# An audio tower on one core: x loaded only in its transposed form, bias by VectorE, more buffers, new instruction orders

## The chip, the cores and the metric

The kernel runs on one core of a Trainium2 chip. The metric is the device time of one execution in microseconds. Three runs of the kernel before gave 224.62, 225.06 and 225.22 us; the median is 225.06 us. The profiled execution took 224.04 us, of which the trace covers a span of 222.3 us.

## What is computed

The input x has 8 sequences of 375 rows of 128 floats. All arithmetic is fp32. Cut to what matters:

```
xt = x^T per sequence
h  = silu(conv1x1(xt, w_compress) + b)             # 128 -> 64 channels
h  = silu(conv3(h, w_main, padding 1) + b)         # 64 -> 64
h  = conv1x1(h, w_expand) + b_expand               # 64 -> 128, the third convolution
y  = layer_norm(h^T + x) * g + b
y  = layer_norm(gelu(y @ w_ff1 + b) @ w_ff2 + b + y) * g + b
h  = max over 3 neighbouring rows                  # 373 rows are left
h  = h + softmax(q k^T) @ n,      n = layernorm(h), q = (n Wq + bq)/sqrt(128), k = n Wk + bk
h  = h + mixture(layernorm(h)):   8 experts 128 -> 256 -> 128 with gelu, the two best of each row,
                                  weighted by a softmax over those two
```

## The kernel before

The work is a set of pieces, each with a name and a number: the number is a sequence (0 to 7), a pair of sequences (0 to 3), or a block. `a1` is the first convolution of a pair, `a2` the second, `a3` the third; `a4` transposes the normalised rows, `a5` and `a6` are the feed-forward part, `a7` transposes back, `mp` is the maximum, `hr` transposes to rows; `b1`, `bq`, `sc0` to `sc2`, `pt0` to `pt2` and `at` are the attention; `h1`, `g1`, `g2`, `g3` the gate of the experts. `l1` to `l4` apply the four layer norms and `p1` to `p4` compute their 1/sqrt on GpSimd.

Three sequences (0, 6, 7) go through all eight experts: `D1` and `D2` are the two products of one expert on TensorE, `dg` the gelu on ScalarE, `da` the weighted sum on VectorE. The five others are sparse. GpSimd scatters their rows (`scat`, 30 indirect DMAs) into a DRAM array by expert, `tab` is the table that tells which 128 rows and which expert each block has, and 37 blocks are computed: SyncE loads the rows (`lx`) and the weights (`lw`, for blocks 8 to 36; `rg` reads one entry of the table into a register first), TensorE transposes (`T`), and multiplies twice (`L1`, `L2`), ScalarE does the gelu (`gl`), VectorE adds the bias (`yv`), and GpSimd scatters the result (`so`). At the end SyncE loads each sparse sequence's results (`yl`), VectorE combines them (`fin`), and SyncE stores (`out`, `od`).

What each engine does next is fixed by five strings, PE_ORDER, DVE_ORDER, ACT_ORDER, POOL_ORDER and SP_ORDER; every engine works through its own string in order and waits on semaphores. In PE_ORDER the figure after the colon is the PSUM bank of the piece. `w.0` to `w.3` are products of the identity with itself whose result nobody reads; WARM says how many (12, 15, 5 and 3). One fp32 matmul shows as two records in the trace (two passes), one transpose as one.

Names that the change touches: x comes in twice, as `xt` (transposed, into `xt_sb`) and as `x` (rows, into `x_sb`, by `load_x` on SyncE's queue). Piece `xb` on GpSimd adds the bias `row_be` of the third convolution to `x_sb` (line 528); piece `a3` on VectorE adds `x_sb` to the convolution's result out of PSUM (line 737). TensorE's `a3` computes a pair of sequences in two banks, 12 matmuls (line 1056). The two lines of SyncE that hold a block's loads back are

```
wait(sp, "T", n - LOADS + 1)            # lx n: ten loads of rows ahead at most
wait(sp, "yv", n + 1 - WSLOTS)          # lw n: seven buffers for weights
```

## Time and profile before

| | before |
|---|---|
| three runs, median (lowest to highest) | 225.06 us (224.62 to 225.22) |
| profiled execution | 224.04 us |
| its span in the trace | 222.3 us |
| TensorE busy | 207.5 us (93%) |
| VectorE busy | 154.3 us (69%) |
| ScalarE busy | 136.8 us (62%) |
| GpSimd busy | 112.7 us (51%) |
| chain that ended last | TensorE 74%, VectorE 8%, ScalarE 5%, DMA 4% |

PE is TensorE's matmuls, PEld its weight loads (which run beside them), DVE VectorE, ACT ScalarE, POOL GpSimd, SPq SyncE's DMA queue. The span falls into a head (0 to about 53 us, the convolutions and the feed-forward part), a middle (53 to 144.75 us, attention and gate), the blocks (144.75 to 199.1 us) and a tail (199.1 us to the end). Idle time of an engine is what stands in brackets in the timeline, with what ended it.

### The profile page before, as it was taken

How to read it: one execution, taken by the hardware profiler on the slowest of the kernel's cores; microseconds unless marked ns; L12 is line 12 of the kernel's file. 1: busy time of each engine (PE TensorE's matmuls, PEld its weight loads, DVE VectorE, ACT ScalarE, POOL GpSimd, SP SyncE). 2: the span in 40 equal slices, each digit the busy share in tenths (PEclk: the TensorE clock that was granted, in tenths of full speed). 3: DMA queues.
4: the chain of work that ended last, by engine and by line, in shares of the span. 5: the costliest groups of instructions: out<-in, count | busy, mean ns of one | idle time of the engine just before them, and what ended most of it. 6: DMA issues, size and time to landing. Idle time of an engine off the chain costs nothing.

```text
span 222.3 us, 5473 instructions
## 1 busy us (share of the span) xinstructions
PE 207.5 (93%) x1575; PEld 170.2 (77%) x1575; DVE 154.3 (69%) x688; ACT 136.8 (62%) x302; POOL 112.7 (51%) x168
## 2 busy tenths in 40 slices
PE   6997897899999999999999999999999799899990
PEld 6875566568956976888779886889998688699780
DVE  6049899999898998988779952486434333234895
ACT  2122988898898588867587446736646366444430
POOL 7608585740541045757774787005777667572000
PEclk9999999999999999999999999999999999999997
DMA  5999999950010002111210121377596889822673
GB/s 152 247 235 288 319 402 406 401 211 3 0 35 0 4 0 69 52 35 58 61 58 25 38 80 48 74 219 251 187 307 225 295 292 322 300 65 76 179 228 105
DMA packets 26000, 35.31 MB, mean 159 GB/s; under 512 B 4083, under 2 KB 18838, under 8 KB 25971
## 3 DMA queue, kind: packets, MB, share of 16 engines
q1 hardware_dynamic: 23137, 30.60, 43.8%
q0 software_dynamic: 2240, 4.00, 5.6%
q10 hardware_dynamic: 594, 0.36, 0.7%
q8 instruction: 13, 0.21, 0.4%
q14 instruction: 16, 0.13, 0.2%
HBM read 10.61 MB, written 14.39 MB: 112 GB/s over the span
## 4 chain that ended last, share of the span: by engine, by line
PE 74%; DVE 8%; ACT 5%; DMA 4%; issue 3%; SPq 3%; POOL 1%; DVEq 0%; ACTq 0%
PE PS L1189 11%; PE PS L1182 10%; PE PS L1124 7%; PE PS L1106 7%; PE PS L1214 5%; PE PS L1001 5%; PE PS L1205 5%; DMA blk_x<-xs 4%; PE PS L989 4%; PE PS L1113 4%; PE PS L1101 3%; PE PS L1018 2%; DVE acc L965 2%; DVE x_sb L930 2%; PE PS L1198 2%
## 5 line engine op out<-in xcount | busy, mean ns | idle before, releaser
L517 POOL TENSOR_TENSOR rstd<-mv,mhalf 125x3 f32<-125x3 f32 x32 | 27.6, 865 | 43.9 <-DVE mv L698 43.7
L547 POOL DMA_INDIRECT ys<-yblk,blk_x x37 | 35.9, 971 | 27.2 <-DVE yblk L956 19.2
L661 ACT ACTIVATE gd<-PS,bias 128x373 f32<-128x373 f32 x48 | 27.0, 573 | 15.4 <-PE PS L1182 10.8
L541 POOL DMA_INDIRECT xs<-rows_x,pos_x x30 | 29.9, 995 | 13.0 <-issue 8.4
L1182 PE MATMUL PS<-xt_sb,w_all 128*128 128x373 f32 x96 | 35.7, 482 | 0.0
L1189 PEld LDWEIGHTS PS<-w_all,gd 128*125 128x125 f32 x288 | 33.6, 187 | 2.1
L1189 PE MATMUL PS<-w_all,gd 128*125 128x128 f32 x288 | 34.6, 273 | 0.0
L672 ACT ACTIVATE gb_t<-PS,blk_w 128x128 f32<-128x128 f32 x58 | 18.0, 364 | 13.3 <-issue 6.9
L930 DVE SCALAR_TENSOR_TENSOR x_sb<-PS,comb,x_sb 125x128 f32<-125x128 f32 x72 | 20.7, 343 | 5.8 <-PE PS L1189 4.9
L1182 PEld LDWEIGHTS PS<-xt_sb,w_all 128*128 128x128 f32 x96 | 15.7, 190 | 5.0 <-issue 0.9
L956 DVE TENSOR_TENSOR yblk<-PS,blk_w 128x128 f32<-128x128 f32 x29 | 8.4, 290 | 15.0 <-PE PS L1214 13.4
L1106 PE MATMUL PS<-xn_t,q_t 128*125 128x373 f32 x48 | 17.7, 486 | 0.0
L1124 PE MATMUL PS<-xn,prob_t 125*125 125x129 f32 (+1 forms) x144 | 17.6, 275 | 0.0
L1214 PE MATMUL PS<-blk_w,gb_t 128*128 128x128 f32 x116 | 17.4, 277 | 0.0
L1205 PE MATMUL PS<-xb_t,blk_w 128*128 128x128 f32 x116 | 17.3, 276 | 0.0
L1124 PEld LDWEIGHTS PS<-xn,prob_t 125*125 125x125 f32 (+1 forms) x144 | 16.7, 187 | 0.8 <-issue 0.4
L1205 PEld LDWEIGHTS PS<-xb_t,blk_w 128*128 128x128 f32 x116 | 15.6, 191 | 1.8 <-issue 0.3
L817 DVE COPY xb_t<-PS 128x128 f32<-128x128 f32 x27 | 7.8, 289 | 13.0 <-PE PS L1198 10.7
L1214 PEld LDWEIGHTS PS<-blk_w,gb_t 128*128 128x128 f32 x116 | 15.0, 191 | 0.7 <-issue 0.3
L831 DVE TENSOR_REDUCE nmax<-PS 125x1 f32<-125x373 f32 x24 | 12.8, 544 | 2.6 <-PE PS L1106 1.8
L637 ACT ACTIVATE prob_t<-PS 124x373 f32<-124x373 f32 (+1 forms) x23 | 9.9, 482 | 6.0 <-PE PS L1113 5.8
L631 ACT ACTIVATE prob<-PS,nmax 125x373 f32<-125x373 f32 x24 | 12.5, 572 | 1.5 <-DVE nmax L831 1.2
(201 smaller groups left out, 416.2 us busy)
## 6 DMA issues: line engine op xcount, KB each, us to landing
blk_w<-w_all SPq DMA_DIRECT2D x29, 321.0 KB, 3.2
xs<-blank SPq DMA_DIRECT2D x1, 8256.0 KB, 25.9
blk_x<-xs SPq DMA_DIRECT2D x37, 64.5 KB
yg<-ys SPq DMA_DIRECT2D x5, 336.0 KB
x_sb<-in_x SPq DMA_DIRECT2D x4, 336.0 KB
out<-x_sb SPq DMA_DIRECT2D x8, 168.0 KB
xt_sb<-in_xt SPq DMA_DIRECT2D x3, 375.0 KB, 6.2
w_all<-in_we SPq DMA_DIRECT2D x1, 1024.0 KB
```

The lines of the kernel that those rows point to most:

```text
L517: pool.tensor_tensor(rstd[i][:, n % 2, :], mv[i][:, n % 2, :, 1], mhalf[:], ALU.pow)\
L541: pool.indirect_dma_start(xs, bass.IndirectOffsetOnAxis(ap=pos_x[:, b // 2, s, i:i + 1], axis=0), rows_x[:, k, s, j, :], None, bounds_chec ...
L547: pool.indirect_dma_start(ys, bass.IndirectOffsetOnAxis(ap=blk_x[n % SLOTS][:, t, D:XW].bitcast(u32), axis=0), yblk[n % YBUF][:, t, :], No ...
L661: act.activation(gd[:, k % GD, c, 0:TP], of("D1", n)[:, 0:TP], ACT.Gelu, bias=bias128[:, 2 + k % E * HC + c:3 + k % E * HC + c]).then_inc( ...
L672: last = act.activation(gb_t[n % 2][:, c, :], of("L1", n)[:, c * BLK:(c + 1) * BLK], ACT.Gelu, bias=w[:, 2 * H + c:2 * H + c + 1])
L930: last = dve.scalar_tensor_tensor(flat(h2[:, b, :])[j], flat(of("D2", n)[0:P, :])[j], w[:, j, b % 2, e:e + 1], flat(h2[:, b, :])[j], ALU.m ...
L1106: pe.matmul(f[0:P, 0:TP], q_t[:, s, OFF[j]:OFF[j] + P], xn_t[:, s, :], start=True, stop=True)\
L1124: last = pe.matmul(f[0:P, j * (D + 1):(j + 1) * (D + 1)], prob_t[0:ROWS[c], s, c, OFF[j]:OFF[j] + P], xn3[0:ROWS[c], s, c, :], start=(c == ...
L1182: pe.matmul(f[:, 0:TP], w_all[:, k % E, c * 128:(c + 1) * 128], x32[:, DENSE[k // E], 0:TP], start=True, stop=True).then_inc(S["D1"], 1)
L1189: last = pe.matmul(f[0:P, j * D:(j + 1) * D], gd[:, n % GD, c, OFF[j]:OFF[j] + P], w_all[:, n % E, H + c * D:H + (c + 1) * D], start=(c == ...
L1205: last = pe.matmul(f[:, c * BLK:(c + 1) * BLK], w[:, c * 128:(c + 1) * 128], xb_t[n % 2][:], start=True, stop=True)
L1214: last = pe.matmul(f[:, t * D:(t + 1) * D], gb_t[n % 2][:, c, t * 128:(t + 1) * 128], w[:, H + c * D:H + (c + 1) * D], start=(c == 0), sto ...
```

## The change

x is no longer loaded as rows. `load_x`, `x_sb` and the GpSimd piece `xb` are gone. TensorE's `a3` now begins with six transposes (three for each sequence of the pair) that put x as rows into the two banks, and the 12 matmuls of the convolution accumulate onto them. VectorE adds the bias `row_be` instead of `x_sb`. The attention's result goes into a tile `h2` of its own.

The room is used for more buffers: 14 for the blocks' weights instead of 7 (seven of them lie in a tile `late` that also holds the attention's `prob` and `prob_t`, so the first load into it waits for the last attention product), 12 for the blocks' results instead of 6, and five for the final loads instead of three, so that `yl` no longer waits for `fin`. WARM goes from (12, 15, 5, 3) to (5, 12, 2, 2). All five orders are new. The code also gets pieces by which ScalarE and GpSimd could take over a `fin`, but no order contains them.

```diff
-WSLOTS = 7
-YBUF = 6
+WSLOTS = 14
+OWN = 7
+YBUF = 12
...
 PE_ORDER = """
-w.0:0 a1.0:5 w.1:0 ft.0:7 a2.0:6 a2.1:3 w.2:0 a3.0:1 a3.1:4 a1.1:3 cb.0:2 w.3:0 a2.2:7 a2.3:6 fn.0:0 a1.2:1 bf.0:4
...
+w.0:0 a1.0:4 w.1:2 a2.0:0 a2.1:1 cb.0:6 ft.0:3 w.2:4 a3.0:2 a3.1:5 a1.1:3 a1.2:6 bf.0:1 a2.2:7 a2.3:4 fn.0:0 w.3:2
...
 POOL_ORDER = """
-xb.0 xb.1 p1.0 p1.1 xb.2 xb.3 xb.4 p1.2 xb.5 p1.3 p1.4 p2.0 p2.1 xb.6 xb.7 p1.5 p1.6 p2.2 p2.3 p3.0 p3.1 p1.7 p2.4
...
+p1.0 p1.1 p1.2 p1.3 p2.0 p2.1 p1.4 p1.5 p1.6 p2.2 p2.3 p3.0 p3.1 p1.7 p2.4 p2.5 p4.0 p2.6 p3.2 p4.1 p3.3 p2.7 p3.4
...
 SP_ORDER = """
-rg.22 rg.23 rg.24 rg.25 rg.26 lx.0 lx.1 lx.2 lx.3 lx.4 lx.5 lx.6 lx.7 lx.8 lw.8 lx.9 lw.9 lx.10 lw.10 lx.11 lw.11
...
+c4.1 c4.2 c4.3 c4.4 rg.8 rg.9 rg.10 lw.8 lw.9 rg.11 rg.12 rg.13 rg.14 rg.15 c4.5 rg.16 lw.10 lw.11 lw.12 rg.17 rg.18
+rg.19 lx.0 lx.1 lx.2 rg.20 rg.21 lx.3 lx.4 lx.5 lx.6 rg.22 lw.13 lx.7 lx.8 lw.14 lx.9 lx.10 rg.23 lx.11 lw.15 lw.16
...
-WARM = (12, 15, 5, 3)
+WARM = (5, 12, 2, 2)
...
-        x_sb = sb("x_sb", [P, B, NJ * D])
...
-        prob = sb("prob", [P, 2, NJ, TP])
+        late = sb("late", [128, (WSLOTS - OWN) * WROW])
+        prob = late[0:P, 0:2 * NJ * TP].rearrange("p (s j t) -> p s j t", s=2, j=NJ)
...
-        prob_t = sb("prob_t", [P, 2, NJ, TE])
-        h2 = x_sb
+        prob_t = late[0:P, 2 * NJ * TP:2 * NJ * (TP + TE)].rearrange("p (s j t) -> p s j t", s=2, j=NJ)
+        h2 = sb("h2", [P, B, NJ * D])
...
             sp.dma_start(xt_sb[:, 0, :], xt[:, 0, :]).then_inc(s_xt[0], 16)
             sp.dma_start(wc_p[:], wc).then_inc(S["wc"], 16)
+            load_xt(1)
             for s in range(2):
                 sp.dma_start(we_d[HALF[s], :], we).then_inc(S["we"], 16)
-            load_x(sp, 0)
-            load_xt(1)
...
-            load_x(sp, 1)
             for q in range(2, Q):
                 load_xt(q)
-                load_x(sp, q)
...
                 if name == "lw":
                     k = n - E
                     if k == 0:
                         sp.wait_ge(S["be1"], 1)
+                    if k == OWN:
+                        wait(sp, "at", B)
...
                 if name == "yl":
-                    if n >= YG:
-                        wait(sp, "ob", n - YG + 1)
...
-                if name == "xb":
-                    pool.wait_ge(s_x[n // 2], 32)
-                    v = x_sb[:, n, :].rearrange("p (j d) -> p j d", j=NJ)
-                    pool.tensor_tensor(v, v, row_be[:].unsqueeze(1).broadcast_to([P, NJ, D]), ALU.add)\
-                        .then_inc(S["xb"], 1)
...
                 if name == "a3":
                     wait(dve, "a3", n + 1)
-                    wait(dve, "xb", n + 1)
+                    if n == 0:
+                        dve.wait_ge(S["rows"], 16)
                     wait_nth(dve, "n1", n - 2)
-                    dve.tensor_tensor(r1[:, n % 2, :], of("a3", n)[0:P, 0:NJ * D], x_sb[:, n, :], ALU.add)\
+                    dve.tensor_tensor(r1[:, n % 2, :].rearrange("p (j d) -> p j d", j=NJ),
+                                      of("a3", n)[0:P, 0:NJ * D].rearrange("p (j d) -> p j d", j=NJ),
+                                      row_be[:].unsqueeze(1).broadcast_to([P, NJ, D]), ALU.add)\
                         .then_inc(S["r1"], 1)
...
                     fs = [claim(name, n - 1, ("r1", n)), claim(name, n, ("r1", n + 1))]
+                    for i in range(2):
+                        for j in range(NJ):
+                            pe.matmul(fs[i][0:P, j * D:(j + 1) * D],
+                                      xt_sb[:, n - 1 + i, :].rearrange("d (p j) -> d j p", j=NJ)[:, j, :], ident[:],
+                                      start=(j == 0), stop=False, is_transpose=True)
                     for j in range(NJ):
                         for i in range(2):
                             for half in range(2):
                                 m = HROWS[half]
                                 last = pe.matmul(fs[i][half * HP:half * HP + m, j * D:(j + 1) * D],
                                                  hc2[HALF[half ^ i], n - 1 + i, j, 0:m], we_d[HALF[half ^ i], :],
-                                                 start=True, stop=True)
+                                                 start=False, stop=(j == NJ - 1))
```

The start of TensorE's order before: the idle products (`PS0<-ident`) stand ahead of the first convolution, ahead of the second, and ahead of the third.

```order
L1001 MATMUL PS0<-ident 128x128 x12
L1007 MATMUL PS5<-xt_sb,wc_p 64x375 x2
L1001 MATMUL PS0<-ident 128x128 x15
L1039 MATMUL PS7<-ident,wk_sb 128x128
L1040 MATMUL PS7<-ident,wq_sb 128x128
L1018 MATMUL PS6<-hc1,wm_d 64x192 x2
...
L1001 MATMUL PS0<-ident 128x128 x5
L1056 MATMUL PS1<-we_d,hc2 64x128
```

The same place now, as far as the first product of the third convolution.

```order
L1026 MATMUL PS0<-ident 128x128 x5
L1032 MATMUL PS4<-xt_sb,wc_p 64x375 x2
L1026 MATMUL PS2<-ident 128x128 x12
L1043 MATMUL PS0<-hc1,wm_d 64x192 x2
...
L1051 MATMUL PS6<-ident,rows6 128x6
L1064 MATMUL PS3<-ident,wk_sb 128x128
L1065 MATMUL PS3<-ident,wq_sb 128x128
L1026 MATMUL PS4<-ident 128x128 x2
L1079 MATMUL PS2<-ident,xt_sb 125x128 x3
L1079 MATMUL PS5<-ident,xt_sb 125x128 x3
L1086 MATMUL PS2<-we_d,hc2 64x128
```

Five, twelve and two idle products are left of twelve, fifteen and five; the transposes of the two weight matrices moved behind the second convolution, and six transposes of `xt_sb` stand ahead of the third.

GpSimd's order at its start before: the bias additions (`x_sb<-x_sb,row_be`) among the 1/sqrt of the first layer norm (`rstd`).

```order
L528 TENSOR_TENSOR x_sb<-x_sb,row_be 125x384 x2
L517 TENSOR_TENSOR rstd<-mv,mhalf 125x3 x2
L528 TENSOR_TENSOR x_sb<-x_sb,row_be 125x384 x3
L517 TENSOR_TENSOR rstd<-mv,mhalf 125x3
L528 TENSOR_TENSOR x_sb<-x_sb,row_be 125x384
L517 TENSOR_TENSOR rstd<-mv,mhalf 125x3
```

The same place now.

```order
L530 TENSOR_TENSOR rstd<-mv,mhalf 125x3 x4
L534 TENSOR_TENSOR nrs<-rstd,minus 125x3
L536 TENSOR_TENSOR nmr<-mv,nrs 125x3
L530 TENSOR_TENSOR rstd<-mv,mhalf 125x3
L534 TENSOR_TENSOR nrs<-rstd,minus 125x3
```

Nothing but the layer norms' small operations is left there.

SyncE's order before, at the first loads of the blocks (`blk_x<-xs` are rows, `blk_w<-w_all` weights, `tab_x` an entry of the table).

```order
L436 DMA blk_x7<-xs 128x129
L436 ISA
L436 DMA blk_x8<-xs 128x129
L444 ISA
L444 DMA blk_w0<-w_all 128x642
L436 ISA
L436 DMA blk_x9<-xs 128x129
L444 ISA
L444 DMA blk_w1<-w_all 128x642
```

SyncE's order now, a little ahead of the first load of rows.

```order
L460 DMA blk_w2<-w_all 128x642
L460 ISA
L460 DMA blk_w3<-w_all 128x642
L460 ISA
L460 DMA blk_w4<-w_all 128x642
L436 TENSOR_LOAD tab_x
...
L450 DMA blk_x0<-xs 128x129
L450 DMA blk_x1<-xs 128x129
L450 DMA blk_x2<-xs 128x129
```

Five loads of weights now stand ahead of the first load of rows, where all of them stood behind the ninth.

## Rows read from the trace of the kernel before

**Rows 1.** Windows: us, then PE, PEld, DVE, ACT, POOL busy, clock, DMA share, GB/s
```profile
15.30:53.17 37.87, 33.53 (x320) 23.18 (x320) 36.12 (x154) 30.07 (x58) 21.81 (x34) 1.00 0.91 306
53.17:144.75 91.58, 91.34 (x614) 73.17 (x612) 73.09 (x371) 67.14 (x134) 46.55 (x60) 1.00 0.14 39
144.75:199.10 54.35, 51.76 (x403) 46.95 (x403) 23.87 (x86) 29.84 (x94) 33.88 (x35) 1.00 0.76 251
```

**Rows 2.** Timeline of the start: start, us, engine, line, operation, idle before
```profile
1.28 0.42 SPq L390 DMA_DIRECT2D wc_p<-in_wc  x1
2.04 5.45 PE L1001 MATMUL PS<-ident 128*128 128x128 f32 x24 [2.04 <-DVE comb_t L712]
2.47 1.41 ACTq L557 DMA_DIRECT2D wm_d<-in_wm  x2
7.43 0.85 PE L1007 MATMUL PS<-xt_sb,wc_p 128*64 128x375 f32 x4
8.21 3.62 PE L1001 MATMUL PS<-ident 128*128 128x128 f32 x30
11.97 1.21 PE L1018 MATMUL PS<-hc,wm_d 64*64 64x192 f32 x24
13.24 0.96 ACT L581 ACTIVATE hc<-PS,bias 128x192 f32<-128x192 f32 x2 [4.28 <-PE PS L1018]
14.42 0.89 PE L1056 MATMUL PS<-we_d,hc 64*64 64x128 f32 x24
```

**Rows 3.** DMA issues: KB each, median us from issue to landing
```profile
wc_p<-in_wc SPq DMA_DIRECT2D x1, 32.0 KB, 3.0
wm_d<-in_wm ACTq DMA_DIRECT2D x2, 48.0 KB, 4.8
```

**Rows 4.** Timeline at 18 to 23 us, VectorE and GpSimd
```profile
18.18 0.82 DVE L704 TENSOR_SCALAR n<-r,mv,rstd 125x128 f32<-125x128 f32 x3
19.17 2.90 POOL L528 TENSOR_TENSOR x_sb<-x_sb,row_be 125x384 f32<-125x384 f32 x3
19.24 2.92 DVE L704 TENSOR_SCALAR n<-r,mv,rstd 125x128 f32<-125x128 f32 x3
```

**Rows 5.** Chain that ended last, pieces: start, us, what
```profile
20.18 1.99 DVE n L704 x2
44.72 0.11 PE PS L1076
170.59 5.03 DMA blk_x<-xs
```

**Rows 6.** Timeline, TensorE where it waits for a block's rows
```profile
175.67 0.33 PE L1198 MATMUL PS<-ident,blk_x 128*128 128x128 f32 x1 [1.40 <-DMA blk_x<-xs]
```

**Rows 7.** Timeline, SyncE's queue among the blocks
```profile
160.01 0.43 SPq L436 DMA_DIRECT2D blk_x<-xs  x1
161.33 0.45 SPq L436 DMA_DIRECT2D blk_x<-xs  x1
166.62 0.51 SPq L444 DMA_DIRECT2D blk_w<-w_all  x1
168.93 0.35 SPq L436 DMA_DIRECT2D blk_x<-xs  x1
192.57 0.58 SPq L444 DMA_DIRECT2D blk_w<-w_all  x1
```

**Rows 8.** Timeline, GpSimd: first and two neighbouring scatters of results
```profile
150.56 0.97 POOL L547 DMA_INDIRECT ys<-yblk,blk_x  x1 [11.91 <-DVE yblk L956]
167.25 0.97 POOL L547 DMA_INDIRECT ys<-yblk,blk_x  x1 [0.30 <-issue]
168.53 0.97 POOL L547 DMA_INDIRECT ys<-yblk,blk_x  x1 [0.30 <-issue]
```

**Rows 9.** Timeline of the tail, VectorE
```profile
207.06 0.87 DVE L930 SCALAR_TENSOR_TENSOR x_sb<-PS,comb,x_sb 125x128 f32<-125x128 f32 x3 [0.45 <-PE PS L1189]
218.87 0.87 DVE L971 SCALAR_TENSOR_TENSOR x_sb<-yg,w_top,acc 125x128 f32<-125x128 f32 x3
```

More of the change, by code:

```diff
@@ L89 @@
+D1.45:1 D2.21:6 D1.46:7 D1.47:4 D2.22:5 D2.23:7
 """
 DVE_ORDER = """
[L91 to L94 removed]
@@ L345, in wait_nth, with summed, gathered, shares @@
                 wait(eng, *nth(name, n))
+        def summed(n):
+            return ("obp", 2 * RANK_POOL["fin", n]) if ("fin", n) in RANK_POOL else ("ob", RANK_DVE["fin", n])
+        def gathered(eng, n):
+            s, loads = s_yl[n]
+            eng.wait_ge(s, loads + 32)
+        def shares(n):
+            return w_top[:, SPARSE[n] // 2, :, :].rearrange("p s (j b) -> p s j b", b=2)[:, :, :, SPARSE[n] % 2:SPARSE[n] % 2 + 1]
         def normed_by(i, n):
@@ L376, in audio_tower @@
         block = ctx.enter_context(nc.Block())
-        def load_x(eng, q):
-            for lo, hi in SPLIT:
-                eng.dma_start(x_sb[lo:hi, 2 * q:2 * q + 2, :],
-                              x[2 * q:2 * q + 2].rearrange("b (p j) d -> p b (j d)", j=NJ)[lo:hi]).then_inc(s_x[q], 16)
         @block.sync
@@ L612, in _ @@
                                    scale=cols[:, 4:5]).then_inc(S[nth("y2", n)[0]], 1)
+                if name == "fm":
+                    gathered(act, n)
+                    w = shares(n)
+                    for s in range(2):
+                        for j in range(NJ):
+                            last = act.activation(flat(yg[n][:, s, :])[j], flat(yg[n][:, s, :])[j], ACT.Copy,
+                                                  scale=w[:, s, j, :])
+                    last.then_inc(S["fm"], 1)
                 if name == "hv":
```

172 lines of the change are left out of this document (90 added, 82 removed).

## Prediction

> **What bounds the kernel now.** I read the busy shares first, then the busy time in stretches, then the chain that ended last, then the timelines at the places where TensorE is idle. TensorE is busy 91.34 of the 91.58 us from 53 us to the blocks. It idles in four places: 2.04 us at the very start [rows 2], 37.87 - 33.53 = 4.34 us in the rest of the head, 54.35 - 51.76 = 2.59 us among the blocks [rows 1], and in the tail, which VectorE ends. Not all of what it does is work. The idle products stand on the chain: 24 records take 5.45 us and 30 take 3.62 us before the second convolution can begin [rows 2]. So an edit counts if it takes something off TensorE, removes one of those waits, or shortens the tail.
>
> **The start.** The first 24 records are spaced 5.45 / 24 = 0.227 us, the next 30 are spaced 3.62 / 30 = 0.121 us. The clock column of the windows says 1.00 for both, but the spacing halves: the engine ran at its lower level of 1.2 GHz from its first instruction until the first convolution began at 7.43, and at 2.4 GHz after it [rows 2]. Now the steps.
> - w.0 has 5 products, 10 records: 10 x 0.227 = 2.3 us, over at 4.3. The weights of the first convolution are issued at 1.28 and land 3.0 us later, at 4.3 [rows 2, 3], and xt at about 4.1. So a1.0 starts near 4.4 instead of 7.4. At the lower clock its 0.78 us (8.21 - 7.43) double to 1.6: over at 6.0.
> - w.1 has 24 records. I take the clock to rise at the same time as before, about 7.5: 7 records at 0.227 (1.6 us) and 17 at 0.121 (2.1 us), over at 9.6. The weights of a2 (issued 2.47 to 3.9, the second about 3.2, landing 4.8 later [rows 2, 3]) are there at 8.0. So a2 starts at 9.6, not 11.97: 2.4 us earlier.
> - After a2 (1.21 us, to 10.8) come three transposes and w.2 with 4 records, about 0.8 us together, beside ScalarE's 0.96 us [rows 2]; the third convolution starts at 11.8. Its six transposes cost 6 x 0.11 [rows 5] = 0.7 us, the products 0.89: it ends at 13.4. Before, it ended at 14.42 + 0.89 = 15.3. Gain so far 1.9 us.
>
> **The lock at 19 us.** VectorE's l1.1 takes 2.92 us, where the same three operations took 0.82 just before; the stretch is exactly that of three bias additions on GpSimd, 19.17 to 22.07 [rows 4]. It is on the chain with 1.99 us [rows 5], and a transpose, the second pair's convolution and ScalarE's work are queued behind it. With xb gone, 2.92 - 0.82 = 2.1 us go. VectorE's new operand, row_be, replaces x_sb in an operation of the same shape that reads PSUM; I cost it at nothing. Bounds: it could lose or gain as much as those operations themselves, 8 x 0.1 us, on an engine that is busy 36.12 of the head's 37.87 us [rows 1].
>
> **What the head pays.** 18 more transposes, 18 x 0.11 = 2.0 us of TensorE in the other three pairs; l2.0 moves from VectorE to ScalarE, which stands on the chain there; w.3 gives 2 records back. There are 4.3 us of waits to hide this in, of which some 1.5 us go with the lock, an estimate from the chain's 1.99 [rows 5]. I take half as exposed: 1.0 us lost, bounds 0 and 2.5. What is late next there is ScalarE, with the gelus and their table loads. The trace has no transposing product whose stationary operand is read with a step of three floats, as x now is. The nearest row is the transpose of contiguous columns at 0.11 us; with a load that takes twice as long it would be 0.22 us, so the 24 cost between 2.6 us and 5.3 us, and less than nothing is excluded since they are added work. I take 0.11, the only row there is.
>
> The Trainium skill speaks against that value: by "SBUF — State Buffer", section "Door 1: The DMA port swizzle", SBUF is read in lines of 16 bytes, full bandwidth wants two hits in a line, and every crossing costs; a step of 12 bytes crosses at almost every element. If it holds for weight loads, the doubled price is nearer. No row of the trace decides it.
>
> **The middle (53 to 144.75 us).** TensorE has 0.24 us of idle time there [rows 1] and the same instructions after the change, only in another order. Nothing is taken off, so a gain carried in stays. I cost the new order at 0, bounds -1 and +1 (VectorE is busy 73.09 of the 91.58 us, so a bad order can open a gap).
>
> **The blocks.** TensorE's gaps come from loads of rows that were issued late: 5.03 us from issue to TensorE [rows 5], with 1.40 us of idle in the largest case [rows 6]. They are issued late because SyncE's queue is nearly full: a pair of loads, rows and weights, takes 161.33 - 160.01 = 1.32 us, and two reads of the table between 166.62 and 168.93 take some 1.6 [rows 7], 0.6 to 0.8 each. Its waits on yv for a weight buffer come on top. With 14 buffers these waits fall away, and five weight loads and twelve table reads stand ahead of lx.0, in a time in which SyncE waited for the last scatter anyway. But the work of that queue from lx.0 on stays: 37 + 24 loads at 0.66 = 40.3 us, 17 table reads at 0.65 = 11.1, od.0 with three stores 1.1, together 52.5. Before, its last load of weights was issued at 193.15 [rows 7], 48.4 us after the blocks began. It starts some 5 us ahead of them, so it is at once the next limit: TensorE's own work is 51.8 us [rows 1], GpSimd's 37 scatters at 168.53 - 167.25 = 1.28 are 47.1 us plus the first 6 us [rows 8]. All three lie within 2 us of each other. Of 2.59 us I take 2.0 as gained, bounds 0 and 2.6. The wait for the last attention product ahead of the first load into `late` queues nothing: that product is over before the blocks begin.
>
> **The tail.** After the last L2, TensorE has 9 D2 and 9 D1 before, and 8 and 11 now; da.19 comes at the same distance. From there VectorE works without a gap, 207.06 to 219.7 [rows 9], and has the same da and fin in the new order. yl no longer waits for fin, but no fin waited for yl. I cost it at 0, bounds -0.5 and +0.5.
>
> **The sum.** 1.9 + 2.1 - 1.0 + 0 + 2.0 + 0 = 5.0 us. Against the profiled execution: 224.0 - 5.0 = 219.0. The median of the runs is 1.0 above that execution, so I forecast a median of 220.0 us. With the bounds: the least gain is 1.9 + 2.1 - 2.5 - 1 + 0 - 0.5 = 0, the most 1.9 + 2.1 + 1 + 2.6 + 0.5 = 8.1.
>
> **Rivals.**
> - *The clock rises late.* With 14 fewer records ahead of a1 the engine has done less when the clock used to rise. If all of w.1 runs at 0.227, it ends at 6.0 + 24 x 0.227 = 11.4, the third convolution at 15.2: the start gives 0.1 instead of 1.9, and the time is 221.8. For it: 24 records and no fewer preceded the rise in the one trace there is [rows 2]. Against: the engine is just as continuously busy now, and time passes equally. By the Trainium skill, "TensorE: Matmul & The Clock Gate", section "What's actually happening", the default is the lower clock and continued activity releases it, whatever the number of matmuls; that is for the forecast. The same page ("Part 4: PE-mode transpose") says that transposes do not count as activity.
> - *SyncE's queue is the bound of the blocks.* Then the 2.0 us don't come, since 52.5 us of issue remain behind lx.0 and a new wait for DMA takes the place of the old one: 222.0. For it, the sum above; against it, that the queue starts earlier relative to TensorE and waits nowhere.
> - *More hides.* The transposes fall into waits and all of the 2.59 us go, and the head's gain is the sum of 1.9 and 2.1, perhaps with a shorter path through ScalarE: 225.1 - 6.6 - 1 = 217.5.
> - *Slower: the strided transposes.* One mechanism: each of the 24 stands on TensorE ahead of a convolution that VectorE waits for. It decides from a price at which they eat the 5.0 us: 0.11 + 5.0 / 24 = 0.32 us each. At 0.4 us, the time is 220.0 + 24 x 0.29 = 227. Against it: the visible weight loads of any kind are under 0.2 us.
> - *The change doesn't do what it says*: the lock stays because GpSimd's small 1/sqrt operations take it too. Against it, l1.0 took 0.82 us [rows 4] although GpSimd computes such a 1/sqrt after every norm; it would cost the 2.1: 222.1.
>
> **Chances.** Forecast (about 219 to 221) 0.40; more hides 0.22; SyncE's queue 0.15; late clock 0.11; lock stays 0.03; strided transposes or a bad gap in the middle, slower than before 0.06; the rest, several small losses, near 224, 0.03. The range from 216.8 to 223.0 leaves out the slower cases and the end of the better ones. A measurement of this kernel can tell about 0.3%, 0.7 us, from no change. Faster by more than that (below 224.4) 0.91, within it 0.03, slower 0.06.
>
> **What would show it.** In the trace after: a1's records at 4.4 us and a2's below 10; the spacing of w.1's records falling from 0.23 to 0.12 inside the piece; three operations of l1.1 at about 0.8 us; the first third convolution ending near 13.4, with its transposes at 0.11 us each; TensorE at the first attention product (53.17 before) about 3.0 us earlier; the first block's transpose about 3 us earlier; no idle over 0.5 us before a block's transpose. Wrong would be: gaps of TensorE on VectorE between 60 and 140 us, SyncE's last weight load less than 4 us earlier, or transposes spaced over 0.2 us.

## The result, and the profile after

The changed kernel takes 223.39 us (median of 13 runs, 222.28 to 224.02), the kernel before beside it 224.62 (13 runs, 223.84 to 227.36): ratio 0.9927, 95% interval [0.9902, 0.9953]. It is faster by 0.7%: 1.2 us in the median and 0.8 in the profiled executions (223.23 against 224.04), where 5.0 were forecast; the time lies outside the forecast range. Medians here and below are over all executions, ratios over those within 1.5% of the fastest of their kernel, so the two can differ.

The start came as forecast. The timeline of TensorE after, which answers to [rows 2] (start, us, engine, line, operation, count, idle before):

```profile
4.45 1.52 PE L1032 MATMUL PS<-xt_sb,wc_p 128*64 128x375 f32 x4
5.90 3.69 PE L1026 MATMUL PS<-ident 128*128 128x128 f32 x24
9.52 1.21 PE L1043 MATMUL PS<-hc,wm_d 64*64 64x192 f32 x24
...
11.79 1.30 PE L1079 MATMUL PS<-ident,xt_sb 128*125 128x128 f32 x6
13.02 0.88 PE L1086 MATMUL PS<-we_d,hc 64*64 64x128 f32 x24
```

The second convolution (a2) starts at 9.52 instead of 11.97. The six new transposes ahead of the third one take 1.30 us; 0.7 were costed. They are spaced (13.02 - 11.79) / 6 = 0.205 us. Their line in the trace after, and the line of the other transposes, which read neighbouring columns, in the trace before (duration in ns as min/median/max, first and last start):

```profile
L1079 PEld LDWEIGHTS PS<-ident,xt_sb x24: 246/258/261, 11.8 to 31.9; 128*125 128x125 f32 x24
```

```profile
L1076 PEld LDWEIGHTS PS<-ident,xt_sb x24: 183/187/188, 26.9 to 59.9; 128*125 128x125 f32 x24
```

Both load 125 columns of 128 partitions in fp32. The one with a step of three floats takes 258 ns, the other 187. The long addition of [rows 4] is gone: VectorE's two groups of three now take 0.82 and 0.86 us (timeline after).

```profile
17.83 0.86 DVE L728 TENSOR_SCALAR n<-r,mv,rstd 125x128 f32<-125x128 f32 x3
```

The blocks after, beside the third of [rows 1] (windows: us, then PE, PEld, DVE, ACT, POOL busy, clock, DMA share, GB/s):

```profile
142.80:196.30 53.50, 50.69 (x401) 46.18 (x400) 23.12 (x80) 30.73 (x100) 33.10 (x34) 1.00 0.71 228
```

TensorE is idle there for 53.50 - 50.69 = 2.81 us, against 2.59 before: that wait didn't go. The two ends of the stretch don't stand at the same work as in [rows 1], since TensorE's order has changed around them (the first block's transpose now stands ahead of the piece `bd.1`, and `D2.15` ahead of the last `L2`). So the whole is compared between two points that have the same work behind them in both, but for one piece of three transposes in another's place: the first attention product and VectorE's addition for da.19. The first of them (timelines of TensorE, before and after):

```profile
53.01 2.16 PE L1124 MATMUL PS<-xn,prob_t 125*125 125x129 f32 x18
```

```profile
52.09 2.16 PE L1154 MATMUL PS<-xn,late 125*125 125x129 f32 x18
```

The head gives 0.92 us, although 2.45 had come in. From there to da.19 (207.06 before in [rows 9], 205.83 after) TensorE has 1081 records in both (windows, before and after):

```profile
53.01:207.06 154.05, 151.22 (x1081) 127.73 (x1080) 100.79 (x471) 99.86 (x234) 82.50 (x97) 1.00 0.37 117
```

```profile
52.09:205.83 153.74, 150.85 (x1081) 127.79 (x1080) 100.62 (x474) 98.82 (x236) 83.40 (x96) 1.00 0.37 117
```

That is 0.31 us less, and the idle time in it is the same: 2.83 us before, 2.89 after. Where it sits among the blocks (timeline of TensorE after, blocks' transposes), and pieces of SyncE's queue, its first load of a block's rows, two later ones and its last load of weights, which answer to [rows 7]:

```profile
186.81 0.33 PE L1228 MATMUL PS<-ident,blank 128*128 128x128 f32 x1 [1.65 <-DMA blank<-xs]
189.02 0.33 PE L1228 MATMUL PS<-ident,blank 128*128 128x128 f32 x1
189.85 0.33 PE L1228 MATMUL PS<-ident,blank 128*128 128x128 f32 x1 [0.50 <-DMA blank<-xs]
```

```profile
138.75 4.50 SPq L450 DMA_DIRECT2D blk_x<-xs  x7
...
186.32 1.95 SPq L450 DMA_DIRECT2D blank<-xs  x2
...
192.25 0.50 SPq L460 DMA_DIRECT2D blk_w<-w_all  x1
```

SyncE issues one thing after the other from its first load of a block's rows at 138.75 us to the last load of weights at 192.25: 53.5 us, in which its waits show none. The queue was nearly as full before: from 140.03 to 192.57 us, 52.5 us, with one wait for a weight buffer (SyncE's waits: us in total, times, longest):

```profile
SPq L444 <- DVE yblk L956: 1.5, 1, 1.5
```

So more buffers had 1.5 us of this queue to save, and the new order put more into the same stretch than it took out: 17 reads of the table instead of 10 and three stores (`od`), for five loads of weights fewer. The chain that ended last runs through SyncE's queue from 178.23 to 187.94 us after.

The tail is as before, 1.2 us earlier: the product for da.19 is added at 205.83 (207.06 in [rows 9]), the last row of the output sums starts at 217.65 (218.87). The end of the span moved by 0.8 only, from 222.3 to 221.5; the last stores took 0.4 us longer in this execution.

### The profile page after: what moved, and what is told of

Its sections match the earlier page's. It is cut to its first block, busy times and chain, and to the rows that moved or that the text cites. A ratio compares the mean times of both kernels' runs of the same rounds, so it can differ in the third digit from the quotient of the medians.

```text
span 221.5 us, 5446 instructions
## 1 busy us (share of the span) xinstructions
PE 208.4 (94%) x1571; PEld 170.8 (77%) x1571; DVE 151.5 (68%) x688; ACT 135.8 (61%) x302; POOL 104.6 (47%) x156
## 4 chain that ended last, share of the span: by engine, by line
PE 79%; DVE 10%; SPq 4%; issue 2%; ACT 1%; DMA 1%; POOL 1%; DVEq 0%
PE PS L1219 12%; PE PS L1212 11%; PE PS L1154 7%; PE PS L1136 7%; PE PS L1235 6%; PE PS L1244 6%; PE PS L1014 4%; PE PS L1143 4%; PE PS L1026 3%; PE PS L1131 3%; PE PS L1079 2%; DVE acc L991 2%; DVE h L957 2%; DVE stat L717 2%; SPq L436 2%
## 5 line engine op out<-in xcount | busy, mean ns | idle before, releaser
L562 POOL DMA_INDIRECT ys<-yblk,blk_x x21 | 20.4, 974 | 19.7 <-DVE yblk L983 15.7
L957 DVE SCALAR_TENSOR_TENSOR h<-PS,comb,h 125x128 f32<-125x128 f32 x72 | 20.8, 344 | 6.8 <-PE PS L1219 5.8
L562 POOL DMA_INDIRECT ys<-yblk,blank x16 | 15.6, 974 | 7.0 <-issue 4.0
L1154 PEld LDWEIGHTS PS<-xn,late 125*125 125x125 f32 (+1 forms) x144 | 16.8, 187 | 1.2 <-issue 0.5
L1154 PE MATMUL PS<-xn,late 125*125 125x129 f32 (+1 forms) x144 | 17.4, 274 | 0.0
L661 ACT ACTIVATE late<-PS 124x373 f32<-124x373 f32 (+1 forms) x22 | 9.6, 481 | 7.6 <-PE PS L1143 7.5
L655 ACT ACTIVATE late<-PS,nmax 125x373 f32<-125x373 f32 x24 | 12.5, 571 | 1.9 <-DVE nmax L858 1.8
L696 ACT ACTIVATE gb_t<-PS,late 128x128 f32<-128x128 f32 x28 | 8.6, 365 | 6.5 <-issue 2.8
L696 ACT ACTIVATE gb_t<-PS,blk_w 128x128 f32<-128x128 f32 x30 | 9.4, 365 | 4.9 <-PE PS L1244 2.5
L717 DVE BATCH_NORM_STATS2 stat<-h 125x6 f32<-125x128 f32 x48 | 10.7, 279 | 0.1
```

Source lines behind the costliest of these rows:

```text
L562: pool.indirect_dma_start(ys, bass.IndirectOffsetOnAxis(ap=blk_x[n % SLOTS][:, t, D:XW].bitcast(u32), axis=0), yblk[n % YBUF][:, t, :], No ...
L696: last = act.activation(gb_t[n % 2][:, c, :], of("L1", n)[:, c * BLK:(c + 1) * BLK], ACT.Gelu, bias=w[:, 2 * H + c:2 * H + c + 1])
L717: dve.bn_stats(stat[i][:, j, 0:6], src[j]).then_inc(s_st[i], 1)
L957: last = dve.scalar_tensor_tensor(flat(h2[:, b, :])[j], flat(of("D2", n)[0:P, :])[j], w[:, j, b % 2, e:e + 1], flat(h2[:, b, :])[j], ALU.m ...
L1154: last = pe.matmul(f[0:P, j * (D + 1):(j + 1) * (D + 1)], prob_t[0:ROWS[c], s, c, OFF[j]:OFF[j] + P], xn3[0:ROWS[c], s, c, :], start=(c == ...
```

## The experiments

Runs of one group share a chip and the runs of the kernel before beside them. The first group (four kernels) fell on a chip where the kernel before takes 225.25 us (223.78 to 228.75, 16 runs), like the chip of the result. The other four groups fell on chips where the same kernel before takes 250.16, 249.63, 250.94 and 250.70 us; what the engines do there from 93 us on is told at the end. Up to that point the traces of all chips agree to 0.1 us once the clock's rise is taken out, so the head is read in all of them and whole times only against the kernel before of the same group.

### The price of the step, and of the transposes

The first edit lets the 24 transposes read neighbouring columns.

```diff
-  xt_sb[:, n - 1 + i, :].rearrange("d (p j) -> d j p", j=NJ)[:, j, :], ident[:],
+  xt_sb[:, n - 1 + i, j * P:(j + 1) * P], ident[:],
```

> The changed kernel, but the 24 transposes of x read 125 neighbouring columns instead of every third one, so the third convolution gets the rows of x in a wrong order; same instructions, same sizes. Theory (the step of three floats makes the weight load slow: 24 transposes at 0.21 us instead of 0.11, and most of the 2.3 us is exposed in the head): spacing 0.11 us, the first attention product 1.5 to 2.3 us earlier than at 52.25, and 1 to 2 us off the total of 223.4, since SyncE's queue then starts earlier too. Rival (what the head loses is the new order of ScalarE and VectorE, and the transposes stand beside it): spacing 0.11 us but the attention product within 0.5 us of 52.25 and the total within 0.5 us.

Measured: 221.47 us (6 runs, 220.97 to 223.31), ratio to before 0.9871 [0.9821, 0.9922]. The weight loads take 187 ns, and six transposes 0.92 us instead of 1.30 (timeline of TensorE):

```profile
8.63 1.21 PE L1043 MATMUL PS<-hc,wm_d 64*64 64x192 f32 x24
10.90 0.92 PE L1079 MATMUL PS<-ident,xt_sb 128*125 128x128 f32 x6
...
49.70 2.16 PE L1154 MATMUL PS<-xn,late 125*125 125x129 f32 x18
```

The first attention product stands at 49.70 where the same view of the changed kernel has 52.09 (the chain dates it 0.16 later). Not all of these 2.4 us belong to the edit: a2 starts 0.9 us earlier here, with the same instructions ahead of it, because the 24 idle products took 2.94 us and not 3.69. The clock rose earlier. So from here on the head is measured from the start of a2 to the first attention product: 52.09 - 9.52 = 42.57 us in the changed kernel, 49.70 - 8.63 = 41.07 in this one. The step costs 1.50 us, 24 x 0.063; all of it is exposed.

What this kernel gains in the head also comes out at the end: da.19 is added at 203.56, 2.27 us earlier than in the changed kernel. SyncE's queue starts and ends earlier by as much (136.32 for 138.75, 189.92 for 192.25):

```profile
136.32 4.67 SPq L450 DMA_DIRECT2D blk_x<-xs  x7
...
189.92 0.50 SPq L460 DMA_DIRECT2D blk_w<-w_all  x1
```

The second edit drops the transposes; the third convolution opens the bank itself, and x is left out of the sum.

```diff
-  for i in range(2):
-      for j in range(NJ):
-          pe.matmul(fs[i][0:P, j * D:(j + 1) * D], xt_sb[...], ident[:],
-                    start=(j == 0), stop=False, is_transpose=True)
...
-                     start=False, stop=(j == NJ - 1))
+                     start=True, stop=True)
```

> The changed kernel without the 24 transposes of x; the third convolution's result goes on without x. Theory: all 24 x 0.21 = 5 us of TensorE go, of which the head shows 3 to 4 us at the first attention product (VectorE and ScalarE are next), and the total falls 2 to 3.5 us, no more since SyncE's queue binds the blocks. Rival (the transposes are hidden): total within 0.7 us.

Measured: 222.74 us (11 runs, 220.56 to 224.93), ratio 0.9882 [0.9842, 0.9923]. In the head it is the shortest: 48.17 - 9.00 = 39.17 us. So 24 transposes with the step cost 3.40 us, 24 without it 1.90; the forecast had 1.7 in its two places. On TensorE itself they take 24 x 0.205 = 4.9 and 24 x 0.142 = 3.4 us, so in both cases 1.5 us of them fell into waits. And yet this kernel is only 0.5 us shorter in span than the changed one (221.0 against 221.5), though its first attention product came 3.9 us earlier. Most of what it gave back stands among the blocks (timeline of TensorE, then of SyncE's queue):

```profile
183.72 0.61 PE L1239 MATMUL PS<-late,gb_t 128*128 128x128 f32 x4
186.96 0.85 PE L1223 MATMUL PS<-ident,blank 128*128 128x128 f32 x2 [2.63 <-DMA blank<-xs]
187.61 1.06 PE L1230 MATMUL PS<-xb_t,late 128*128 128x128 f32 x4
```

```profile
134.88 4.22 SPq L450 DMA_DIRECT2D blk_x<-xs  x7
...
182.52 2.13 SPq L450 DMA_DIRECT2D blank<-xs  x2
...
189.03 0.50 SPq L460 DMA_DIRECT2D blk_w<-w_all  x1
```

SyncE again needs 189.03 - 134.88 = 54.2 us from its first load to its last. Its first load came 3.9 us earlier than in the changed kernel, its last 3.2, and the two loads of rows at 182.52 are 3.8 us ahead of the same ones there (186.32). So the queue kept nearly all of the gain; what came late was the data. TensorE could use the first of the two 4.4 us after its issue (186.96 - 182.52), in the changed kernel 2.7 us after it (189.02 - 186.32). Why it landed late isn't shown. TensorE waited 2.63 us, and then ran four products in 1.06 us that had taken 0.61: the granted clock was 0.50 from 188 to 190 us. From the first attention product to da.19 this kernel takes 155.95 us, 2.2 more than the changed one (windows):

```profile
48.17:204.12 155.95, 152.50 (x1081) 129.44 (x1080) 100.65 (x475) 98.83 (x236) 83.29 (x96) 0.99 0.36 113
```

Of these 2.2 us, 0.56 are idle time (3.45 against 2.89) and 1.65 are the same products taking longer. In the tail VectorE then waited 0.8 us for its final loads. This is one execution; the kernel's eleven lie between 220.56 and 224.93 us.

### SyncE's queue

The 29 reads of the table of rows are replaced by the numbers that they give for these inputs. It is no kernel to use, since the numbers hold for these inputs alone, but every transfer stays as it is.

```diff
+FIXED = [CAP * e + BLK * (k + 1) for e, m in enumerate((1, 0, 8, 9, 0, 6, 3, 0)) for k in range(m)] + 2 * [ROWS_X - BLK]
...
-  row_of_block[n] = sp.value_load(tab_x[0:1, n - E:n - E + 1], min_val=0, max_val=ROWS_X - BLK)
+  row_of_block[n] = FIXED[n - E]
```

> The changed kernel, with the 29 reads of the block table on SyncE replaced by the numbers that stand in the table for these inputs. All DMAs stay the same. Theory (the blocks are bound by the number of things SyncE issues one after another): SyncE's last weight load is issued 5 us or more earlier than 192.3, TensorE's 2.8 us of idle among the blocks go, total 2 to 2.8 us lower. Rival (the blocks are bound by what the DMA engines move, 0.71 to 0.8 of them being busy): idle before the blocks' transposes stays over 2 us, total within 0.7 us.

Measured: 219.33 us (6 runs, 218.74 to 219.77), ratio 0.9752 [0.9711, 0.9792], so 4.0 us less than the changed kernel by the two ratios. The head is the changed one (51.84 - 9.27 = 42.57 us). Among the blocks the idle time is gone (windows; the second line is from the first attention product to da.19), and SyncE has time (its queue, and its waits up to 181.7 us as us in total, times, longest):

```profile
142.80:196.30 53.50, 53.45 (x428) 49.53 (x429) 23.95 (x84) 32.27 (x103) 34.90 (x36) 1.00 0.70 227
51.84:202.22 150.38, 150.19 (x1081) 127.79 (x1080) 100.66 (x475) 98.76 (x236) 83.31 (x96) 1.00 0.37 119
```

```profile
138.45 3.61 SPq L451 DMA_DIRECT2D blk_x<-xs  x7
...
181.71 0.47 SPq L461 DMA_DIRECT2D blk_w<-w_all  x1
```

```profile
SPq L451 <- DMA xs<-rows_x,pos_x: 11.8, 1, 11.8
SPq L461 <- DVE yblk L984: 3.0, 5, 1.7
SPq L451 <- PE PS L1229: 3.0, 6, 0.9
SPq L376 <- DMA ys<-yblk,blk_x: 2.0, 2, 1.6
```

From the first attention product to da.19 it is 150.38 us instead of 153.74, 3.36 less, of which 2.70 are idle time (0.19 for 2.89). The rest of the 4.0 is the clock's earlier rise (0.25) and 0.4 us of stores at the very end. First load to last load is 43.3 us instead of 53.5, although SyncE now waits 8.0 us in it, for VectorE, TensorE and GpSimd's scatters: its own work fell from 53.5 to 35.3 us. The edit removes more than the 17 reads behind the first load: with constants, the register operations that work out each load's address go as well, so the 18.2 us are the price of both. Ahead of the first load SyncE waits 11.8 us for the last scatter, where the changed kernel's waited 1.8. So the reads filled the time before the blocks as well.

Both edits together:

> Both edits: transposes of neighbouring columns, and no table reads on SyncE. Theory: the two gains add, 3.5 to 4.8 us below the changed kernel, which would be what the forecast missed. Rival (either bound hides behind a third, GpSimd's scatters at 1.28 us a block): less than 2.5 us together.

Measured: 217.69 us (6 runs, 217.42 to 217.97), ratio 0.9678 [0.9639, 0.9716]: 0.0074 under the constants alone, 1.7 us, which agrees with the 1.50 of the step. With the table reads in place the step had been worth 0.0056, 1.3 us; the intervals don't tell these two apart. TensorE has no idle time in 142.80 to 196.30 (53.50 busy). The two losses add up. At 0.9678 this kernel is some 7 us faster than the kernel before, more than the 5.0 that the forecast expected of the change itself.

### The parts of the head, on the kernel before

Only the shorter idle products:

```diff
-WARM = (12, 15, 5, 3)
+WARM = (5, 12, 2, 2)
```

> The kernel before with the changed kernel's idle products alone (5, 12, 2 and 2 instead of 12, 15, 5 and 3). If the earlier start is worth what the changed trace shows there, the first convolution begins near 4.5 us, the second near 9.5, the first third convolution ends near 13.0 instead of 15.3, and the first attention product stands near 51 instead of 53.2: median near 223. If the later waits of the head (the 2.9 us addition beside GpSimd, ScalarE's gelus) are set by something other than TensorE's start, the first attention product stays within 0.7 us of 53.2 and the median near 224.8.

Only the additions on GpSimd taken away, x left out:

```diff
-  pool.wait_ge(s_x[n // 2], 32)
-  v = x_sb[:, n, :].rearrange("p (j d) -> p j d", j=NJ)
-  pool.tensor_tensor(v, v, row_be[:].unsqueeze(1).broadcast_to([P, NJ, D]), ALU.add).then_inc(S["xb"], 1)
+  continue
...
-  dve.tensor_tensor(r1[:, n % 2, :], of("a3", n)[0:P, 0:NJ * D], x_sb[:, n, :], ALU.add)
+  dve.tensor_tensor(r1[...], of("a3", n)[...], row_be[:].unsqueeze(1).broadcast_to([P, NJ, D]), ALU.add)
```

> The kernel before without GpSimd's eight additions of the bias to x; VectorE adds the bias row to the product instead, and x itself is left out of the sum. If the 2.9 us operation at 19 us is a collision with those additions, it falls to 0.8 us and the first attention product comes 1.5 to 2 us earlier: median near 223. If the chain through ScalarE takes over there, the operation is short but the first attention product moves less than 0.7 us: median near 224.7.

Both:

> Both of the edits above: fewer idle products, and no additions on GpSimd (x left out of the sum). It is the changed head without its transposes. If the two gains add up, the first attention product stands near 49.5 us and the median near 221. If they cover the same time, it stands near 51 and the median near 223. The difference to the changed kernel's 52.25 us is what 24 strided transposes cost in the head: 2.7 us or more by the theory that they are exposed at 0.20 us each, 1.3 or less by the forecast's 0.11 us half hidden.

Whole times, on a chip with the kernel before at 250.16 us: 246.89 (12 runs), ratio 0.9979 [0.9927, 1.003]; 247.32 (12), 0.9986 [0.9937, 1.0036]; 243.29 (8), 0.9845 [0.9783, 0.9907]. The intervals are too wide for the totals to decide; the heads are exact. The starts of a2 and of the first attention product, in the timelines of these three in turn:

```profile
9.85 1.21 PE L1018 MATMUL PS<-hc,wm_d 64*64 64x192 f32 x24
...
50.72 2.16 PE L1124 MATMUL PS<-xn,prob_t 125*125 125x129 f32 x18
```

```profile
11.51 1.21 PE L1019 MATMUL PS<-hc,wm_d 64*64 64x192 f32 x24
...
51.20 2.16 PE L1125 MATMUL PS<-xn,prob_t 125*125 125x129 f32 x18
```

```profile
9.01 1.21 PE L1019 MATMUL PS<-hc,wm_d 64*64 64x192 f32 x24
...
48.53 2.16 PE L1125 MATMUL PS<-xn,prob_t 125*125 125x129 f32 x18
```

| kernel | a2 starts | first attention product | between |
|---|---|---|---|
| before | 11.97 | 53.01 | 41.04 |
| before, idle products as changed | 9.85 | 50.72 | 40.87 |
| before, no additions on GpSimd | 11.51 | 51.20 | 39.69 |
| before, both | 9.01 | 48.53 | 39.52 |
| changed | 9.52 | 52.09 | 42.57 |
| changed, neighbouring columns | 8.63 | 49.70 | 41.07 |
| changed, no transposes | 9.00 | 48.17 | 39.17 |

The additions cost 41.04 - 39.69 = 1.35 us, and 40.87 - 39.52 = 1.35 again beside the other edit. VectorE's operation itself fell from 2.92 to 0.86 us in both (timeline of the second of these kernels):

```profile
18.77 0.86 DVE L701 TENSOR_SCALAR n<-r,mv,rstd 125x128 f32<-125x128 f32 x3
```

Only 1.35 of these 2.06 us reached the path because TensorE had the second pair's convolution to do in the meantime. Before, it then waited 1.28 us for this operation; without the additions it doesn't wait (timelines of TensorE, before and this kernel):

```profile
20.05 0.88 PE L1056 MATMUL PS<-we_d,hc 64*64 64x128 f32 x24
22.21 0.54 PE L989 MATMUL PS<-ident,n 125*128 125x125 f32 x3 [1.28 <-DVE n L704]
```

```profile
20.40 0.54 PE L990 MATMUL PS<-ident,n 125*128 125x125 f32 x3
```

The column adds up: 41.04 - 0.17 (shorter w.2 and w.3) - 1.35 (additions gone) - 0.35 (the rest, the new orders and l2.0 on ScalarE, from 39.52 to 39.17) + 1.90 (24 transposes) + 1.50 (their step) = 42.57.

### The kernel before without its table reads

This is the constants' edit on the kernel before.

> The kernel before with its 29 reads of the table of rows replaced by the same numbers as constants. If SyncE's queue was already the bound of the blocks before, most of TensorE's 2.6 us of idle time there goes and the median is near 222.5. If the waits for a weight buffer set it (9 buffers), the reads fall into those waits and the median stays within 0.7 us of the kernel before.

> Again the kernel before with its 29 reads of the table replaced by constants, beside the others on one chip. If SyncE's queue bounded the blocks before too, TensorE's 2.6 us of idle time there falls under 1 us and the median is near 222.5 (ratio 0.988). If the waits for a weight buffer, with 9 of them, set it, the ratio is over 0.997.

> The kernel before with its 29 reads of the table replaced by constants, once more. If SyncE's queue bounded the blocks before too, TensorE's 2.6 us of idle time there falls under 1 us and the ratio is near 0.988. If the waits for a weight buffer, with 9 of them, set it, the ratio is over 0.997.

> The kernel before with its 29 reads of the table replaced by constants. If SyncE's queue bounded its blocks, its idle time of 2.6 us there falls under 1 us and the ratio is 0.985 to 0.99. If the waits for one of its 9 weight buffers do, over 0.997. On a chip that takes 250 us for the kernel before, the ratio is 0.98 to 0.99 as in the last groups.

Measured on four chips: 0.9829 [0.9734, 0.9923], 0.9888 [0.9821, 0.9956], 0.9801 [0.9715, 0.9886] and 0.9772 [0.9693, 0.9851] (246.14, 245.55, 249.66 and 245.92 us, 6, 12, 6 and 7 runs). All four intervals lie below 1, so the reads and addresses cost the kernel before 1 to 2% as well. But all four chips are of the kind that takes 250 us, and how the gain comes about there isn't shown: in the profiles taken on them, with the reads or without, TensorE waits for no block's rows at all, and SyncE waits for one of its seven weight buffers (the expectations say nine) for 8.9 us in the kernel with the shorter idle products and for 16.9 in the first one with constants. On a chip that takes 225 us this edit wasn't seen, and what it does to the 2.6 us of idle time stays open.

### A version without both losses and without constants

The step can be had for nothing. The host lays xt out with the time steps of one residue side by side; the transposes then read neighbouring columns, and ScalarE puts the order back when it evicts the first convolution.

```diff
-  "xt": a(x, 2, 0, 1),
+  "xt": a(np.asarray(x).reshape(B, P, NJ, D), 3, 0, 2, 1).reshape(D, B, T),
...
-  act.activation(hc1[:, n % 2, 1:T + 1], of("a1", n)[:, 0:T], ACT.Silu, bias=bias64[:, 0:1])
+  act.activation(hc1[:, n % 2, 1:T + 1].rearrange("c (p j) -> c p j", j=NJ),
+                 of("a1", n)[:, 0:T].rearrange("c (j p) -> c p j", j=NJ), ACT.Silu, bias=bias64[:, 0:1])
```

> The changed kernel with xt laid out so that the time steps of one residue (mod 3) are neighbours: the 24 transposes read contiguous columns, and ScalarE's first activation of each pair reads its input with a step of 125 floats instead, to put the order back. Output as the reference's. If the step of 12 bytes in the stationary load is what the transposes paid for, they are spaced 0.11 us, the first attention product comes about 2 us earlier than in the changed kernel (near 50.2), and the median is 1.5 to 2 us under the changed kernel's (near 221.5, ratio to before near 0.985), as with the run on neighbouring columns. If the strided read only moves its price to ScalarE's first activation (0.96 us before), that operation grows and the gain is under 0.7 us.

> The changed kernel with xt laid out by residue, once more. In the head it was 1.5 us shorter than the changed kernel, at the same instruction order. If that reaches the end, the median is 1.5 us under the changed kernel's and the ratio near 0.986. If SyncE's queue, which starts its block loads only 2 us after the last scatter allows, holds the blocks, part of it goes: ratio near 0.991.

The queue can be relieved by issuing the rows of the first eight blocks, whose addresses are fixed, in two transfers.

```diff
+  if n < E:
+      if n in GROUP:                      # {0: (0, 2), 2: (2, 8)}
+          lo, hi = GROUP[n]
+          sp.dma_start(first8[:, lo:hi, :], xs.rearrange("(n r) d -> r n d", n=E)[0:BLK, lo:hi, :])\
+              .then_inc(s_bx[lo], 16)
+      continue
```

> The changed kernel with the loads of rows of the first eight blocks, whose addresses are fixed, issued as two DMAs (blocks 0 and 1, blocks 2 to 7) instead of eight. If what SyncE issues one after the other is the bound of the blocks, six issues fewer at 0.66 us put its last load of weights 3 to 4 us earlier (192.25 before this edit), TensorE's idle time of 2.8 us in the blocks nearly goes, and the median is 2 us lower, near 221.4. If the bytes or the landing time of single loads set it, the median stays within 0.7 us of the changed kernel's 223.4, or is worse where block 2 waits for six blocks at once.

> The changed kernel with the first eight blocks' rows in two DMAs, once more. Serial issue as the bound: the last load of weights 3 to 4 us earlier relative to the first load of rows, TensorE's idle time in the blocks under 1 us, ratio near 0.985. Bytes or landing as the bound: ratio within 0.003 of 0.993.

And both together:

> Both of the edits above in the changed kernel, output as the reference's and nothing taken from the inputs' values. If the two losses are independent, as the two kernels with wrong order and with constants made it look, about 219.5 (ratio to before near 0.975). If a third limit close behind (GpSimd's 37 scatters, or TensorE itself) holds the blocks, about 221.

> Layout and two DMAs together, once more: near 219.5 us, ratio near 0.976, if the losses are independent; 0.985 if one limit is behind both.

> The changed kernel with xt laid out by residue and the first eight blocks' rows in two DMAs, output as the reference's. On a chip that runs the kernel before in 225 us: from the second convolution to the first attention product 41.07 us instead of 42.57, SyncE's last load of weights 3.7 us nearer to its first load of rows than the 53.5 us of the changed kernel, median near 219.5, ratio near 0.975. If one more limit holds the blocks, 221.5. On a chip that takes 250 us the ratio is between 0.995 and 1.005, as in the last two groups.

In their own places both edits do what they should. The layout's head is 50.44 - 9.38 = 41.06 us, 1.51 less than the changed one, and the same to 0.02 us in its second run and in the three runs of both together; with the two transfers alone it is 42.57 and 42.58. ScalarE's activation with the step of 125 floats in PSUM costs nothing (groups of line, operation, shape | busy, mean ns; the layout's and the changed kernel's):

```profile
L592 ACT ACTIVATE hc<-PS,bias 128x375 f32<-128x375 f32 x4 | 2.3, 573 | 3.9 <-PE PS L1033 2.6 <-DMA bias<-in_b 1.2
```

```profile
L592 ACT ACTIVATE hc<-PS,bias 128x375 f32<-128x375 f32 x4 | 2.3, 575 | 4.2 <-PE PS L1032 3.0 <-DMA bias<-in_b 1.1
```

The two transfers bring SyncE to its ninth load of rows sooner. In the layout's kernel that is the second of the pair at 151.57, at 152.39, 7.2 us after the first load at 145.15; with the two transfers it is 3.5 us after it (145.72 to 149.21, SyncE's queue in the two kernels).

Whole times show none of it. The layout: 248.81 us, ratio 1.0055 [0.9995, 1.0116], and 252.23, 1.0045 [0.9972, 1.0119]. Two transfers: 250.14, 1.0066 [0.9964, 1.0169], and 253.46, 1.013 [1.0062, 1.0197]. Both: 247.92, 0.9968 [0.9916, 1.002], then 252.19, 1.0034 [0.9961, 1.0108], then 248.81, 1.0011 [0.996, 1.0061]. The two transfers could hardly show there, since TensorE waits for no block's rows in any profile of these chips. So on these chips the changed kernel's descendants are not faster than the kernel before, though they reach the first attention product 0.6 to 3.3 us ahead of it. Whether the version with both takes about 219.5 us on a chip like the first stays open: neither was seen there. The best time of a kernel with the table read from the device and x in its right order is therefore the changed kernel's own.

## Why the prediction was wrong

- **The start: right.** a1 was forecast at 4.4 us and came at 4.45; w.1 was to be over and a2 to start at 9.6, and it started at 9.52. The late clock didn't come: the spacing still halves inside w.1. What was not foreseen is that this moment moves between executions. In the fourteen profiles of kernels with the same idle products a2 starts between 8.49 and 9.87 us.
- **Six transposes at 0.11 us: wrong.** They take 1.30 us instead of 0.7, and the third convolution ends at 13.90, not 13.4. The 0.11 us of [rows 5] is a piece of the chain at a single transpose, not the spacing of a series, and it wasn't the only row there is: before, three transposes of `n` in a row, from neighbouring columns, are spaced (20.05 - 19.58) / 3 = 0.157 us (timeline of TensorE before; the next line starts at 20.05).

```profile
19.58 0.54 PE L989 MATMUL PS<-ident,n 125*128 125x125 f32 x3
```

- **"What the head pays", 1.0 us: the mis-sized term.** With the start's 0.7 the forecast had 1.7 us for 24 transposes; they cost 3.40 us. What failed is the price of one, 0.205 us instead of 0.11. The share taken as exposed was nearly right: 1.5 of the 4.9 us fell into waits, and with the measured price the forecast's own way of counting (the first six in full, half of the other 18) gives 1.2 + 1.8 = 3.1 us. The prediction named the missing price and both bounds (2.6 to 5.3 us in all), and took the cheap end. It had also named a spacing over 0.2 us as a sign that it was wrong, and that sign came.
- **The Trainium skill's rule was the better guide.** By "SBUF — State Buffer", section "Door 1: The DMA port swizzle", crossings of 16-byte lines cost. The trace agrees in direction: 258 against 187 ns for a load with a step of 12 bytes. It doesn't give the doubling that the prediction worked out from it: six transposes go from 0.92 to 1.30 us, a factor of 1.4.
- **The lock, 2.1 us: mechanism right, size too large.** The operation fell from 2.92 to 0.86 us as forecast, and 1.35 us reached the path. The whole shortening of the operation was taken as the gain, with the chain's 1.99 us of [rows 5] for support, but TensorE was busy with a convolution for the first part of it and waited 1.28 us; only that wait could go.
- **The middle, 0: right.** TensorE's idle time there was 0.24 us before and is 0.08 after (90.55 - 90.47 from 52.25 to 142.80 us).
- **The blocks, 2.0 us: the second failed step.** 0.3 us came, and none of it from the idle time, 2.83 us before and 2.89 after. The prediction summed SyncE's work behind lx.0 to 52.5 us, found it above TensorE's own 51.8, and still took the gain. It was 53.5 us. It didn't make the same sum for the kernel before, where it is 52.5 us with a single wait of 1.5: more weight buffers could take away only that, and the last load of weights is issued 0.3 us earlier than before, where less than 4 had been named as a sign of being wrong. The rival "SyncE's queue is the bound of the blocks" was right, at a chance of 0.15. Relieving that queue of reads and address arithmetic removed the idle time and 4.0 us. The sum for GpSimd is slightly off (37 x 1.28 = 47.4, not 47.1), and nothing hangs on it.
- **The tail, 0: right**, but for 0.4 us of stores at the very end that no step named.

In sum, in the profiled executions: head 0.9 instead of 3.0, middle and blocks 0.3 instead of 2.0, end -0.4 instead of 0, so 0.8 instead of 5.0. Two optimistic choices between bounds that had been written down, and 0.75 us too much for the lock, made the difference, and the range was too narrow because it let them fail only one at a time.

## What to carry to other kernels

Where a serial queue of issues feeds an engine, sum what it issues between two fixed points and compare that with the busy time of the engine; if they are within a few per cent, and the queue hardly waits, more buffers don't help. Make the sum for the kernel before as well, and look at what a new order adds to it. A gain ahead of such a queue comes out only as far as the queue's own start moves with it, as it did here with neighbouring columns (2.4 us in the head, 2.3 at da.19). A stationary operand read with a step pays per product (0.063 us here), and the repair may be a layout on the host plus a strided eviction that costs nothing. And when the clock's rise moves between executions, measure a stretch from an event behind the rise, not from the start.

## What the runs showed of the hardware

- A weight load of 125 fp32 columns costs 187 ns from neighbouring columns and 258 ns with a step of 12 bytes; the products behind it are spaced 0.142 and 0.205 us.
- ScalarE reads PSUM with a step of 125 floats at the price of neighbouring ones, 573 against 575 ns.
- One read of the table takes 0.5 us of SyncE's queue by the medians of its records, as much as issuing a load of weights. In the trace it is three records of the sequencer (ns as min/median/max), none of them busy time of an engine:

```profile
L436 SPq TENSOR_LOAD <-tab_x x29: 263/322/875, 122.0 to 186.7; - x29
L436 SPq FUSED_REGOPS  x29: 147/155/192, 122.5 to 187.5; - x29
L436 SPq SEQ_ASSERT  x29: 18/18/37, 122.7 to 187.7; - x29
```

- A wait of 2.6 us inside a stretch that had been busy was followed by the lower clock (granted clock 0.50 from 188 to 190 us, four products in 1.06 us instead of 0.61), in one execution. The wait of 1.65 us in the changed kernel wasn't: four products behind it take 0.61 us.
- The chips differ by a tenth in this kernel. The chips on which it takes 250 us keep step with the others to 0.1 us until about 93 us. Then several engines stand still together for 1 to 5 us at a time, and by the end the layout's kernel is 27 us behind the one with neighbouring columns. The first such place in the layout's kernel (timeline; the same instructions of the one with neighbouring columns, on the faster chip, start at 90.30 and 90.48 us, without these waits):

```profile
93.06 0.33 DVE L905 TENSOR_TENSOR one<-iota_e,topi 125x48 f32<-125x48 uint32 x2 [2.05 <-remote]
93.38 1.23 ACT L662 ACTIVATE late<-PS 124x373 f32<-124x373 f32 x3 [2.68 <-remote]
```

  VectorE and ScalarE begin 2.05 and 2.68 us after their last work, released by nothing that the profile names. The cause wasn't found. It matters for the verdict: the gain of 0.7% is that of the faster chips, and on the others no version of the changed kernel that was run is ahead of the kernel before by more than the measurement's uncertainty.
